# Edge MLP of a graph network on one core: two of the three bf16 parts of h as one stationary operand of 128 columns, and TensorE's loop over two slabs in place of four

## What is computed

```python
edge_input = jnp.concatenate([x[src], x[dst], edge_attr, u[batch[src]]], axis=-1)
h = jax.nn.relu(edge_input @ W1 + b1)                       # 200000 x 64
agg = jax.ops.segment_sum(h, dst, num_segments=x.shape[0])  # 6250 x 64
new_input = jnp.concatenate([x, agg, u[batch]], axis=1)
return jax.nn.relu(new_input @ W2 + b2)
```

## Time and profile before

| | |
|---|---|
| median of 3 runs | 7745.59 us (7742.32 to 7759.3) |
| the profiled execution | 7743.19 us |
| its span, first to last instruction | 7741.5 us |
| granted TensorE clock, mean over the span | 0.81 |
| PE / PEld / DVE / ACT / POOL busy | 72% / 57% / 42% / 17% / 28% |
| edge MLP stage | about 3486 to 6147 us of the span |

### The profile page before, as it was taken

One profiled execution on the slowest core, in us unless ns is written; L12 is line 12 of the kernel. 1 busy time (PEld: TensorE's weight loads), 2 busy tenths in 40 slices (PEclk: granted clock), 3 DMA queues, 4 the chain that ended last, 5 costly groups with the idle time before them and its releaser, 6 DMA issues.

```text
span 7741.5 us, 161418 instructions
## 1 busy us (share of the span) xinstructions
PE 5600.9 (72%) x52264; PEld 4422.3 (57%) x52265; DVE 3277.2 (42%) x5887; ACT 1350.9 (17%) x3492; POOL 2142.1 (28%) x3521
## 2 busy tenths in 40 slices
PE   0999988777777799945555655656555599789956
PEld 0777776666666799944555545545555544334455
DVE  7899888777777310132222222222222300200043
ACT  0122234555555200010000000000000000000010
POOL 1222222222222000005555555555555300000000
PEclk9999999999999899975555555555555599899978
DMA  1011223343444489852222222222222299679755
GB/s 32 20 52 52 77 73 121 114 134 122 136 138 135 163 352 388 343 119 55 58 57 57 58 58 59 60 56 60 60 57 60 58 301 300 226 255 298 257 203 219
DMA packets 427400, 1053.65 MB, mean 136 GB/s; under 512 B 126711, under 2 KB 283713, under 8 KB 398401
## 3 DMA queue, kind: packets, MB, share of 16 engines
q1 hardware_dynamic: 377090, 1000.81, 38.9%
q0 software_dynamic: 50176, 51.48, 3.9%
HBM read 809.69 MB, written 242.41 MB: 136 GB/s over the span
## 4 chain that ended last, share of the span: by engine, by line
PE 55%; another core or an unknown queue 15%; DVE 14%; issue 8%; POOLq 2%; ACT 2%; ACTq 1%; DMA 1%; DVEq 1%; POOL 0%; SPq 0%; PEldq 0%; PEld 0%
PE banks L1498 15%; PE banks L1528 14%; PE banks L1459 10%; PE banks L1422 5%; PE banks L1490 4%; PE banks L1431 3%; DVE T L805 3%; DVE T L812 2%; POOLq L336 2%; ACTq L332 1%; PE banks L1417 1%; DVE WORK L882 1%; PE banks L1418 1%; PE banks L1419 1%
## 5 line engine op out<-in xcount | busy, mean ns | idle before, releaser
L599 POOL DMA_INDIRECT WORK<-table,idx x1568 | 1501.5, 958 | 2023.1 <-DVE idx L900 890.3
L1498 PE MATMUL banks<-T 128*128 128x125 bf16 (+1 forms) x21696 | 1669.4, 226 | 41.3 <-DVE T L812 6.3
L1498 PEld LDWEIGHTS banks<-T 128*128 128x128 bf16 x21696 | 1442.9, 115 | 336.7 <-DVE T L812 321.9
L805 DVE TENSOR_TENSOR T<-T 128x750 bf16<-128x750 bf16 x1808 | 999.9, 553 | 391.7 <-PE banks L1498 309.5
L1528 PE MATMUL banks<-T,WORK 125*64 125x400 f32 (+1 forms) x3200 | 1056.6, 493 | 45.4 <-ACT WORK L1327 41.5
L556 POOL TENSOR_TENSOR T<-T 128x12 f32 x1816 | 560.0, 308 | 1770.5 <-DVE T L812 1252.4
L812 DVE TENSOR_TENSOR T<-T 128x750 bf16<-128x750 bf16 x1808 | 1000.7, 553 | 62.1
L1490 PE MATMUL banks<-T 128*128 128x250 bf16 x3616 | 710.1, 277 | 363.7 <-DVE T L805 124.9
L1431 PE MATMUL banks<-WORK 128*64 128x128 bf16 x4704 | 628.3, 299 | 451.3 <-issue 447.1
L1459 PE MATMUL banks<-WORK,T 125*128 125x192 bf16 (+1 forms) x10000 | 833.1, 247 | 63.1 <-DVE WORK L944 63.1
L1459 PEld LDWEIGHTS banks<-WORK,T 125*128 125x128 bf16 (+1 forms) x10000 | 830.8, 99 | 65.4 <-issue 47.3
(11 more groups left out here) (336 smaller groups left out, 3466.7 us busy)
## 6 DMA issues: line engine op xcount, KB each, us to landing
T<-dense_c SPq DMA_DIRECT2D x200, 1562.5 KB, 8.4
T<-dense_w SPq DMA_DIRECT2D x300, 800.0 KB, 4.3
dense_w<-WORK SPq DMA_DIRECT2D x250, 546.9 KB
T<-dense_w SPq DMA_DIRECT2D x100, 725.0 KB, 4.2
WORK<-rel_rows SPq DMA_DIRECT2D x197, 256.0 KB
WORK<-in_eaT SPq DMA_DIRECT2D x196, 256.0 KB
dense_c<-T SPq DMA_DIRECT2D x13, 3125.0 KB, 10.6
dense_c<-ACC SPq DMA_DIRECT2D x12, 3125.0 KB, 10.8
```

The source lines that it names most:

```text
L599: nc.gpsimd.indirect_dma_start(out=g_sb[:, u, c * D:(c + 1) * D], out_offset=None, in_=table, in_offset=bass.IndirectOffsetOnAxis(ap=idx[: ...
L805: V.tensor_tensor(planes[:, v, 0:HOTS].rearrange("p (k n t) -> p k n t", k=3, t=QUAD), iota2[:, 0:LO, :].unsqueeze(1).to_broadcast([P, 3, ...
L1498: last = T.matmul(banks[:, u, to - low // QUAD:to + LO + high // QUAD], keys[:, t, j, :], planes[:, v, first - low:past + high].rearrange( ...
```

## The change

The first two parts of h now lie side by side, chunk by chunk (`parts12`), so that one 128x128 stationary operand carries both: their products come out on partitions 0 to 63 and 64 to 127 of the bank. The third part (`parts3`) keeps matmuls of its own, which accumulate on partitions 0 to 63. So 24 window matmuls of a slab become 16. `add_window` adds 128 partitions, the memset clears all of `ACC_full`, and the product after the stage contracts over 128 partitions with `W2b` stacked twice, which sums the two halves. ACT's first ReLU and DVE's three operations on the parts write and read with one more level in their patterns; their sizes stay. TensorE's loop body holds two slabs in place of four.

```diff
-        parts = WORK[:, 2048:3584].bitcast(BF16).rearrange("p (s k n) -> p s k n", s=2, k=3)
+        parts12 = WORK[:, 2048:3072].bitcast(BF16).rearrange("p (s c k f) -> p s c k f", s=2, c=CHUNKS, k=2)
+        parts3 = WORK[:, 3072:3584].bitcast(BF16).rearrange("p (s c f) -> p s c f", s=2, c=CHUNKS)
...
-            def begin_rounds():
-                V.memset(ACC[:], 0.0).then_inc(round_set, 1)
+            def begin_rounds(sums):
+                V.memset(sums, 0.0).then_inc(round_set, 1)
...
+                def by_chunk(t, w):
+                    return t[:, w, :].rearrange("p (c f) -> p c f", f=D)
...
-                        V.tensor_tensor(ACC[:, ds(pos, P)], ACC[:, ds(pos, P)], banks[0:D, u % 2, 0:P], ALU.add).then_inc(slabs_free, 1)
+                        V.tensor_tensor(ACC_full[:, ds(pos, P)], ACC_full[:, ds(pos, P)], banks[:, u % 2, 0:P], ALU.add).then_inc(slabs_free, 1)
...
-                            V.tensor_tensor(g_sb[:, w, :], g_sb[:, w, :], parts[:, v, 0, :], ALU.subtract).then_inc(parts_step, 1)
+                            V.tensor_tensor(by_chunk(g_sb, w), by_chunk(g_sb, w), parts12[:, v, :, 0, :], ALU.subtract).then_inc(parts_step, 1)
...
-                            V.tensor_copy(parts[:, v, 1, :], g_sb[:, w, :]).then_inc(parts_step, 1)
+                            V.tensor_copy(parts12[:, v, :, 1, :], by_chunk(g_sb, w)).then_inc(parts_step, 1)
...
-                            V.tensor_tensor(parts[:, v, 2, :], g_sb[:, w, :], parts[:, v, 1, :], ALU.subtract).then_inc(parts_ready, 1)
+                            V.tensor_tensor(parts3[:, v, :, :], by_chunk(g_sb, w), parts12[:, v, :, 1, :], ALU.subtract).then_inc(parts_ready, 1)
...
-                        C.activation(parts[:, u % 2, 0, :], g_sb[:, u, :], ACT.Relu)
+                        C.activation(parts12[:, u % 2, :, 0, :], g_sb[:, u, :].rearrange("p (c f) -> p c f", f=D), ACT.Relu)
...
                     for c in range(CHUNKS):
-                        for k in range(3):
-                            last = T.matmul(banks[0:D, v, 0:P], parts[:, v, k, c * D:(c + 1) * D], hots[:, v, c // 2, :, c % 2],
-                                            start=c == 0 and k == 0, stop=c == CHUNKS - 1 and k == 2, skip_group_check=True)
+                        T.matmul(banks[:, v, 0:P], parts12[:, v, c, :, :].rearrange("p k f -> p (k f)"), hots[:, v, c // 2, :, c % 2], start=c == 0, stop=False, skip_group_check=True)
+                    for c in range(CHUNKS):
+                        last = T.matmul(banks[0:D, v, 0:P], parts3[:, v, c, :], hots[:, v, c // 2, :, c % 2], start=False, stop=c == CHUNKS - 1, skip_group_check=True)
...
                 def turn(r, i, first):
-                    at = loads(pe, pos_i[0:1, 0:RING] if first == 0 else pos_i[0:1, ds(i * RING + first, RING)], 0, DUMP)
-                    for u in range(first, first + RING):
+                    at = loads(pe, pos_i[0:1, 0:2] if first == 0 else pos_i[0:1, ds(i * 2 + first, 2)], 0, DUMP)
+                    for u in range(first, first + 2):
...
-                    with pe.Fori(0, TURNS - 1) as i:
-                        turn(r, i, RING)
+                    with pe.Fori(0, SLABS // 2 - 1) as i:
+                        turn(r, i, 2)
...
-                    last = T.matmul(banks[0:LO, g, (t - first) * D:(t - first + 1) * D], ACC[:, t * LO:(t + 1) * LO], W2b, start=True, stop=True, skip_group_check=True)
+                    last = T.matmul(banks[0:LO, g, (t - first) * D:(t - first + 1) * D], ACC_full[:, t * LO:(t + 1) * LO], W2b_twice, start=True, stop=True, skip_group_check=True)
```

More of the change, by code:

```diff
@@ L219, in gnn_kernel @@
         mat = sb("mat", [P, 12 * D])
-        W1c, W1d, W2b, W2c = (mat[0:D, i * D:(i + 1) * D] for i in (6, 7, 9, 10))
+        W1c, W1d, W2c = (mat[0:D, i * D:(i + 1) * D] for i in (6, 7, 10))
+        W2b_twice = mat[:, 9 * D:10 * D]
         W01, W23, WL3 = mat[:, 0:D], mat[:, 2 * D:3 * D], mat[:, 11 * D:12 * D]
@@ L833, in edge_pass @@
                 RB, PB = before(dve, p, R)
-                begin_rounds()
+                begin_rounds(ACC[:])
                 def one_hots(first, slot):
@@ L856, in mlp_pass @@
                 RB, PB = before(dve, 3, R)
-                begin_rounds()
+                begin_rounds(ACC_full[:])
+                def by_chunk(t, w):
+                    return t[:, w, :].rearrange("p (c f) -> p c f", f=D)
                 def turn_hots(v, loaded):
@@ L1412, in z_of @@
                     v, at = u % 2, pos * (D // ALIGN)
-                    pe.wait_ge(hotsT_ready, r * (SLABS + 1) + i * RING + (u + 2))
-                    pe.wait_ge(zsum_ready, r * SLABS + i * RING + (u + 1))
+                    pe.wait_ge(hotsT_ready, r * (SLABS + 1) + i * 2 + (u + 2))
+                    pe.wait_ge(zsum_ready, r * SLABS + i * 2 + (u + 1))
                     for c in range(CHUNKS):
@@ L1419, in z_of @@
                         T.matmul(z, lhsT, QW3[:, ds(at, D)], start=False, stop=False, skip_group_check=True)
-                    pe.wait_ge(ea_loaded[v], (r * (SLABS // 2) + i * (RING // 2) + (u // 2 + 1)) * 16)
+                    pe.wait_ge(ea_loaded[v], (r * (SLABS // 2) + i + (u // 2 + 1)) * 16)
                     for c in range(CHUNKS):
@@ L1425, in windows_of @@
                 def windows_of(r, i, u):
-                    v, n = u % 2, slab_no(RB, r, i, u)
-                    pe.wait_ge(parts_ready, r * SLABS + i * RING + (u + 1))
+                    v, n = u % 2, (r + RB) * SLABS + i * 2 + u
+                    pe.wait_ge(parts_ready, r * SLABS + i * 2 + (u + 1))
                     pe.wait_ge(slabs_free, n + 1 + (RING - 2))
                     for c in range(CHUNKS):
-                        for k in range(3):
-                            last = T.matmul(banks[0:D, v, 0:P], parts[:, v, k, c * D:(c + 1) * D], hots[:, v, c // 2, :, c % 2],
-                                            start=c == 0 and k == 0, stop=c == CHUNKS - 1 and k == 2, skip_group_check=True)
+                        T.matmul(banks[:, v, 0:P], parts12[:, v, c, :, :].rearrange("p k f -> p (k f)"), hots[:, v, c // 2, :, c % 2], start=c == 0, stop=False, skip_group_check=True)
+                    for c in range(CHUNKS):
+                        last = T.matmul(banks[0:D, v, 0:P], parts3[:, v, c, :], hots[:, v, c // 2, :, c % 2], start=False, stop=c == CHUNKS - 1, skip_group_check=True)
                     last.then_inc(windows_ready, 1)
                 def turn(r, i, first):
-                    at = loads(pe, pos_i[0:1, 0:RING] if first == 0 else pos_i[0:1, ds(i * RING + first, RING)], 0, DUMP)
-                    for u in range(first, first + RING):
+                    at = loads(pe, pos_i[0:1, 0:2] if first == 0 else pos_i[0:1, ds(i * 2 + first, 2)], 0, DUMP)
+                    for u in range(first, first + 2):
                         z_of(r, i, u, at[u - first])
```

## The result

| | before | change |
|---|---|---|
| median, same chip | 7748.94 us | 7818.99 us (7811.1 to 7828.46) |
| ratio | | 1.009 (95% interval 1.0072 to 1.0107) |
| profiled execution, its span | 7743.19, 7741.5 us | 7811.1, 7809.3 us |
| granted TensorE clock | 0.81 | 0.796 |
| edge MLP stage | 2660.8 us | about 2733.7 us |

What follows compares the result with a forecast made beforehand. The prediction took the edge MLP to be bound by late `z_ready`, PE's instructions filling a queue that empties slowly while POOL gathers. 149 + 49 = 198 us less than 7743.19 gave 7545 us, range 7050 to 7760.

Steps and rivals of the forecast that it cites:

- Stalled windows: Window matmuls (L1431) in slow slabs: 1568 fewer at 95 ns of "issue" idle each, 149 us less.
- What fills it is the number of PE instructions: Edge MLP: while POOL issues gathers, PE's queue empties slowly, and PE's instruction count fills it until issue stalls.
- Quiet windows: Window matmuls in fast slabs: 16 in place of 24, 0.5 us less on every second slab, 49 us.
- Slabs alternate: Edge MLP stage: a fast slab of 7.15 us is followed by a slow one of 20.5 us.
- "no change" rival: Edge MLP: POOL's pause alone ends the stall, period stays two slabs of gathers and one pause; 7743 us, chance 0.13.
- slower rival: DVE's cast L892 loses its pace in the interleaved pattern, 53 us, and stalls don't shrink; 7796 us, chance 0.12.
- three pattern edits: DVE's operations on the parts get one more pattern level: costed at nothing, worst case 53 us at L892.
- short loop: PE's loop body: a shorter one removes the stalls altogether and POOL's floor binds; 7063 us, chance 0.18.
- Loads of 128 columns: PE's weight loads: 128 columns taken as no dearer than 64, from 121 ns against 159, stalls included.
- The range: Whole kernel: 7050 us (loop rival) to 7760 (no change with the runs' spread), leaving out the slower rival.

Runs made afterwards that it cites:

- no_third: The change without the eight window matmuls a slab of the third part: 7814.73 us, 1.007 times the kernel before.
- late_add_before: The kernel before with `add_window` moved behind the copy to `idx`, so its wait no longer holds up the index hand-out: 7845.94 us, 1.0043.
- separate_two: The kernel before with PE's loop over two slabs in place of four, 24 window matmuls kept: 7819.82 us against 7813.09, 1.0007.
- before_again: The kernel before, unedited, run again with a profile on a chip without stalls: 7085.17 us against 7080.69, 1.0009.
- paced_half: The change with two POOL memsets of 256 columns put in as a pause behind every fourth gather: 7506.35 us, 0.9684 times the kernel before.

## Why the prediction was wrong

**"Stalled windows", 149 us: this term failed**, and with it the reading "What fills it is the number of PE instructions". It divided 447.1 us of "issue" idle by 4704 matmuls and took the 95 ns for a price. They are no price. `no_third` took away another 1568 matmuls and gained 6 us; the change itself has 755 us of such idle on fewer matmuls. The delay lasts as long as POOL issues gathers without a pause, and `z_ready` comes 2.6 to 3.0 us after POOL's last one in the trace after. I had both facts in hand (L881 came 9.8 us behind z's last matmul, 2 us behind POOL's last gather) and still let the count of PE's instructions set the length.

**"Quiet windows", 49 us: right as a saving, wrong as a gain.** The windows did fall from 2.77 to 2.0 us. A fast slab keeps its 7.3 us all the same (7.15 before), from L886 at 3624.32 to 3631.59, since the chain is DVE's and z's; the saving lies beside it. Stretches of two slabs didn't get shorter either (27.74 us, 27.66 before). The term was at its lower end of 0.

**What was left out: +70 us.** "Slabs alternate" was read from two slabs; 31 of the 79 stretches that I measured hold three. I costed `add_window`'s line by its 277 ns alone and never asked about the 353.7 us of wait ahead of it and what is queued behind that: L897 and so POOL. With the wait goes the short pause that it made. Three-slab stretches of 13.16 us a slab turn into two-slab ones of 13.87. `late_add_before` brings the same lock and a loss of 0.43% without any merge. That the lock costs the whole 70 us is a sum from two traces (66 us), and no run put the short pause back into the change by way of DVE's wait.

**The "no change" rival had the mechanism.** It gave the period as two slabs of gathers and one pause, 20 and 6.84 us. That is the change's rhythm, 27.74 us for two slabs with a pause of 7.8. It missed only that the kernel before was not wholly in that rhythm (27.66 us for 48 stretches, and 31 of three slabs that are better).

**The slower rival had the sign and not the reason.** The cast kept its pace, 421 ns beside 426, and so did the subtraction, 692 beside 697. The three pattern edits, `add_window` over 128 partitions (282 beside 277 ns) and the memset (5392 ns both times) cost nothing, as said.

**The short loop did nothing.** The change's body, 242 instruction records of PE in its trace, has more "issue" idle (931 us) than the long one (677), and `separate_two` stands at 1.0007. The times near 7063 did appear, but for both kernels and with the chip or the hour, not with the loop: in `before_again` the long body, 543 records, doesn't stall at all.

**Loads of 128 columns** cost 127 ns beside 150 for 64, stalls included, as the prediction took it from the earlier trace rows. By the Trainium skill, "TensorE: Matmul & The Clock Gate", section "LDWEIGHTS (loading the stationary operand)", the time would grow with the columns; these rows don't show it, and the quiet windows fell with the count of matmuls.

**The range** ended at 7760 and left the slower case out at 0.12. Both PE terms had one sign because nothing was allowed for a rhythm that changes.

**Open.** What inside the chip holds PE back, and why three sets of runs don't show it, no run tells. Each of the five chips of the experiments was used in one set of runs only, and the sets with stalls came first, so the chip and the hour aren't told apart. Within a set it was steady: the kernel before lay between 7740 and 7770 us in all runs of one. Also open is the shortest pause that frees PE; the shorter ones ran only where there was nothing to free. Whether pauses are worth having depends on the stalls: `paced_half` took 3.2% less with them, the same pauses in the kernel before 5.9% more without them, so no version that beats both kernels everywhere was found.

## What to carry to other kernels

A wait that ends on something other than its own producer can't be costed by counting the producer's instructions: find whose activity ends it, and vary that. Before removing a wait, ask what is queued behind it on its engine, and whether the delay of that is what keeps another engine from crowding a third; here the removed wait made the pauses that the rest lived on. And compare a tuned kernel on more than one chip, and at more than one time, before believing in a bound: here stalls worth 9%, which came and went with the set of runs, hid that POOL's eight gathers a slab are the floor.

## What the runs showed of the hardware

- While POOL issued indirect gathers back to back (0.94 us each, 0.30 between), PE's instructions came out in small groups with 0.5 to 1.7 us between them, and PE's semaphores were raised late. In the profile after, the one at the end of z came 2.6 to 3.0 us after the end of POOL's last gather in 95 of 96 late cases, once 12.1 us behind PE's last matmul (3639.88 to 3652.01). In the profile before, 11 of 80 late ones came while POOL was still issuing.
- With fewer PE instructions PE no longer stalled itself (`no_third`, 68 us of "issue" idle in place of 931), and the semaphore came as late as before (1587.9 us of wait beside 1558.5).
- A gap of 1.13 to 1.65 us in place of 0.30 after every fourth gather removed it: 7506.35 beside 7756.98 us.
- It isn't always there. The kernel before took 7813 and 7757 us in two sets of runs on two chips, and 7084, 7081 and 7088 us in three later sets on three others, with durations of POOL's gathers (957 and 958 ns) and of PE's quiet pieces (3.67 and 2.77 us) that don't differ.
